# Weight pieces awaited at their first product, attention weights by columns, and new orders on every engine of a transformer block kernel

## The chip, the cores and the metric

One NeuronCore of a Trainium2 chip runs one program. The metric is the device time of one execution in microseconds (us). TensorE multiplies matrices (PE in the rows; PEld is its load of the stationary operand), VectorE (DVE), ScalarE (ACT) and GpSimd (POOL) work elementwise, and SyncE (SP) issues every DMA.

## What is computed

Eight sequences of 256 rows by 256 columns pass through a half-weighted feed-forward layer, an attention layer and a second half-weighted feed-forward layer, each after a layer norm and each added to its input:

```python
x = L0_attn_x                                             # 8 x 256 x 256
x = x + 0.5 * ffn(layernorm(x), w_gate, w_up, w_down)     # hidden 1024, silu(gate) * up
x = x + attn(layernorm(x), gamma, w_qkv, w_out)           # 16 query heads, 4 key heads of 64
x = x + 0.5 * ffn(layernorm(x), w_gate, w_up, w_down)
```

`attn` scales each row to norm 16 with `gamma`, projects to q, k and v (1536 columns), turns q and k by rotary angles, applies a causal softmax, and projects back with `w_out`.

## The kernel before

**Split operands.** Every weight and activation is held as two rounded parts, "hi" and "lo", and a product is three matmuls: hi by hi, lo by hi, hi by lo (`product`, L979). The lo part is a subtraction that ScalarE's rounding copy must precede.

**Work items.** Each engine runs a hand-written list of small functions, one list for the opening (first sequence, and the first layer of the second), one for the loop (six turns; each does the attention of one sequence, the second feed-forward of the same, and the first feed-forward of the next), and one for the ending. On TensorE `gate()`, `up()` and `down()` are twelve matmuls each (L979); pair number F of the hidden layer takes one gate, one up and one down. Four pairs make a layer. `x_transposes` (L988) turn a normed input, `qkv` (opening, ending: by rows) or `qk` and `value_rows` (loop: by columns) are the attention's projections, then come `q_transposes` (opening, ending), `scores`, `p_transposes`, `values` and `projection`.

**Chains between engines.** Feed-forward: gate (PE), `tanh` (ACT, L602), `gate_product` (DVE, L860, which frees the gate's bank and so releases the next gate), up (PE), `up_product` (DVE, L868), `hidden_hi` (ACT, L610), `hidden_lo` (POOL, L436), down (PE). Attention, for eight groups n of four heads: scores, (`low_copy` on ACT, `low_mask` on POOL for the first four groups in the loop), `mask_max` (DVE), `exps` (ACT), `inverse` (DVE), `normalise` (POOL), `p_transposes` (PE), `p_hi` (ACT), `p_lo` (DVE), values (PE), and for two groups together `outputs_hi`, `outputs_lo`, then projection. Layer norm: `statistics` (DVE), `powers` (POOL, four small operations), `normal_rows` (ACT), x_transposes (PE), `x_hi` (ACT), `x_lo` (DVE).

**Rotary.** In the loop `rope_products` (DVE), `rope_add` (POOL), `rope_hi` (ACT) and `rope_lo` (DVE for jobs 0 and 1, POOL for 2 to 4) end in 24 DMAs that restack k and q (`k_restack`, `q_restack` on SP). In the opening and ending `row_products` (DVE) and `row_add` (POOL) precede the q_transposes.

**Weights.** Twelve pieces are loaded into four staging slots: 0 to 3 gate, up, gate, up (first and second half of the hidden layer), 4 and 5 down, 6 to 9 qkv, 10 and 11 out. A piece is rounded by ACT (`split_hi`, L499) and subtracted by DVE (`split_lo`, L673, L675) or, for 4, 5, 10 and 11, by POOL (L342). SP issues piece i when piece i - 4 is subtracted (`lo_done`). TensorE's list has six waits on the counts of finished pieces written into it.

All order comes from these lists and the semaphores between them; nothing is planned at run time.

## Time and profile before

| | before |
|---|---|
| median of 3 runs | 579.34 us (577.7 to 579.7) |
| the profiled execution, own time | 579.26 us |
| its span, first to last instruction | 577.5 us |
| outside the span | 1.8 us |
| TensorE busy / granted clock | 556.5 us (96%) / 0.991 |
| DVE, ACT, POOL busy | 419.9, 379.5, 373.2 us |
| opening / six turns / ending, by first q, k or v product | 99.2 / 397.7 / 80.7 us |

An engine's busy time counts its instructions' modelled spans; matmuls overlap, so two matmuls that start 0.11 us apart are each shown 0.28 us long. Where a wait is shorter than that overlap, only the distance of two starts tells it.

### The profile page before, as it was taken

How to read it: one execution, taken by the hardware profiler on the slowest of the kernel's cores; microseconds unless marked ns; L12 is line 12 of the kernel's file. 1: busy time of each engine (PE TensorE's matmuls, PEld its weight loads, DVE VectorE, ACT ScalarE, POOL GpSimd, SP SyncE). 2: the span in 40 equal slices, each digit the busy share in tenths (PEclk: the TensorE clock that was granted, in tenths of full speed). 3: DMA queues.
4: the chain of work that ended last, by engine and by line, in shares of the span. 5: the costliest groups of instructions: out<-in, count | busy, mean ns of one | idle time of the engine just before them, and what ended most of it. 6: DMA issues, size and time to landing. Idle time of an engine off the chain costs nothing.

```text
span 577.5 us, 13669 instructions
## 1 busy us (share of the span) xinstructions
PE 556.5 (96%) x4364; PEld 528.7 (92%) x4364; DVE 419.9 (73%) x1207; ACT 379.5 (66%) x1013; POOL 373.2 (65%) x410
## 2 busy tenths in 40 slices
PE   7779999999999999999999999999999999899997
PEld 4778999999999999999999999999999999789997
DVE  3686986859867695867867697767868698698533
ACT  4543893479836896379935897368934897479422
POOL 1645562886849775795839875697749877545322
PEclk9897999999999999999999999999999999999999
DMA  7340000250005200160004300070003400000001
GB/s 227 115 132 2 2 1 20 70 151 2 20 18 151 67 18 0 55 182 0 18 18 117 101 17 1 21 200 15 18 18 87 131 0 0 19 1 2 1 1 37
DMA packets 28090, 29.70 MB, mean 51 GB/s; under 512 B 2976, under 2 KB 25888, under 8 KB 28064
## 3 DMA queue, kind: packets, MB, share of 16 engines
q1 hardware_dynamic: 28064, 29.37, 18.3%
q8 instruction: 14, 0.23, 0.2%
q14 instruction: 12, 0.10, 0.1%
HBM read 8.39 MB, written 2.10 MB: 18 GB/s over the span
## 4 chain that ended last, share of the span: by engine, by line
PE 77%; DVE 7%; SPq 5%; issue 4%; ACT 2%; POOL 2%; DMA 2%; POOLq 0%; ACTq 0%; DVEq 0%
PE bank L979 51%; PE bank L988 9%; PE bank L1113 6%; PE bank L1083 5%; SPq L296 3%; PE bank L1108 3%; PE bank L1079 2%; SPq L285 2%; DVE hid L860 1%; DVE q_t L754 1%; ACT hid L602 1%; DMA q_t<-rotated 1%; DMA eye_sb<-in_eye 1%; POOL out_lo L342 1%; DVE qkv_lo L675 1%
## 5 line engine op out<-in xcount | busy, mean ns | idle before, releaser
L427 POOL TENSOR_TENSOR probs<-probs,inv_sum 128x512 f32<-128x512 f32 (+1 forms) x64 | 93.9, 1470 | 54.0 <-DVE inv_sum L828 53.9
L570 ACT ACTIVATE probs<-probs,neg_max 128x128 f32<-128x128 f32 (+1 forms) x256 | 113.2, 450 | 3.9 <-DVE neg_max L818 3.7
L436 POOL TENSOR_TENSOR hid_lo<-hid,hid_hi 128x512 fp32r<-128x512 f32 x64 | 82.8, 1298 | 33.7 <-ACT hid_hi L610 33.0
L979 PE MATMUL bank<-xf_t_hi,gate_hi 128*128 128x256 f32 x256 | 75.1, 293 | 6.9 <-DVE gate_lo L673 3.8
L979 PE MATMUL bank<-down_hi,hid_hi 128*128 128x256 f32 x256 | 72.9, 285 | 1.3 <-POOL hid_lo L436 1.2
L979 PE MATMUL bank<-xf_t_hi,up_hi 128*128 128x256 f32 x256 | 72.9, 285 | 0.0
L979 PE MATMUL bank<-down_hi,hid_lo 128*128 128x256 f32 x256 | 71.8, 280 | 0.0
L979 PE MATMUL bank<-xf_t_hi,up_lo 128*128 128x256 f32 x256 | 71.8, 280 | 0.0
L979 PE MATMUL bank<-down_lo,hid_hi 128*128 128x256 f32 x256 | 71.8, 280 | 0.0
L979 PE MATMUL bank<-xf_t_lo,up_hi 128*128 128x256 f32 x256 | 71.8, 280 | 0.0
L979 PE MATMUL bank<-xf_t_lo,gate_hi 128*128 128x256 f32 x256 | 71.6, 280 | 0.0
L979 PE MATMUL bank<-xf_t_hi,gate_lo 128*128 128x256 f32 x256 | 71.5, 279 | 0.0
L602 ACT ACTIVATE hid<-bank 128x512 f32<-128x512 f32 x64 | 38.2, 597 | 49.7 <-PE bank L979 39.2
L860 DVE SCALAR_TENSOR_TENSOR hid<-hid,bank 128x512 f32<-128x512 f32 x64 | 43.7, 683 | 28.1 <-ACT hid L602 27.8
L979 PEld LDWEIGHTS bank<-xf_t_hi,gate_hi 128*128 128x128 f32 x256 | 48.3, 189 | 10.9 <-DVE gate_lo L673 4.0
L818 DVE CUSTOM_DVE_ANT_0 probs<-bank,mask_sb 128x256 f32<-128x256 f32 (+1 forms) x160 | 55.3, 390 | 0.9 <-PE bank L1083 0.5
L988 PE MATMUL bank<-eye_sb,probs 128*128 128x128 f32 x384 | 52.0, 273 | 0.2
L979 PEld LDWEIGHTS bank<-down_hi,hid_hi 128*128 128x128 f32 x256 | 48.7, 190 | 2.6 <-POOL hid_lo L436 1.6
L446 POOL TENSOR_TENSOR o_t_lo<-o_sums,o_t_hi 128x512 fp32r<-128x512 f32 x24 | 31.1, 1294 | 30.6 <-ACT o_t_hi L595 30.6
L868 DVE TENSOR_TENSOR hid<-hid,bank 128x512 f32<-128x512 f32 x64 | 43.9, 685 | 9.1 <-PE bank L979 6.2
L570 ACT ACTIVATION_READ_ACCUMULATOR probs<-probs,neg_max 128x1 f32 x256 | 49.9, 195 | 0.0
L979 PEld LDWEIGHTS bank<-down_lo,hid_hi 128*128 128x128 f32 x256 | 48.8, 191 | 0.6
(142 smaller groups left out, 1809.3 us busy)
## 6 DMA issues: line engine op xcount, KB each, us to landing
q_t<-rotated SPq DMA_DIRECT2D x96, 128.0 KB, 2.6
k_t<-rotated_k SPq DMA_DIRECT2D x48, 128.0 KB, 2.6
x_in<-in_x SPq DMA_DIRECT2D x7, 256.0 KB, 2.7
out<-y_out SPq DMA_DIRECT2D x7, 256.0 KB, 2.1
probs<-in_w_qkv SPq DMA_DIRECT2D x4, 384.0 KB, 3.7
probs<-in_w_gate SPq DMA_DIRECT2D x2, 512.0 KB, 6.7
probs<-in_w_up SPq DMA_DIRECT2D x2, 512.0 KB, 7.6
probs<-in_w_down SPq DMA_DIRECT2D x2, 512.0 KB, 4.5
```

Of the source, the lines that this page charges most:

```text
L427: nc.gpsimd.tensor_tensor(part, part, inv_sum[:, slot].unsqueeze(2).broadcast_to([P, GROUP, keys]), ALU.mult).then_inc(p_done, 1)
L436: nc.gpsimd.tensor_tensor(hid_lo[:, slot].rearrange("p c n -> p (c n)"), hid[:, slot], hid_hi[:, slot].rearrange("p c n -> p (c n)").bitca ...
L446: nc.gpsimd.tensor_tensor(o_t[1][:, t, jp].rearrange("p g s -> p (g s)"), o_sums[:], o_t[0][:, t, jp].rearrange("p g s -> p (g s)").bitcas ...
L570: last = nc.scalar.activation(part, part, ACT.Exp, bias=neg_max[:, slot, g:g + 1], scale=-1.0, accum_out=row_sum[:, slot, g:g + 1])
L602: nc.scalar.activation(hid[:, slot], bank[G_BANK][:], ACT.Tanh, scale=0.5).then_inc(th_done, 1)
L818: last = nc.vector.tensor_tensor_reduce(part, bank[S_BANKS[pair]][:, g % 2 * SEQ:g % 2 * SEQ + keys], mask_sb[:, SEQ - keys:SEQ] if masked ...
L860: nc.vector.scalar_tensor_tensor(out=hid[:, slot], in0=hid[:, slot], scalar=1.0, in1=bank[G_BANK][:], op0=ALU.add, op1=ALU.mult).then_inc( ...
L868: nc.vector.tensor_tensor(hid[:, slot], hid[:, slot], bank[U_BANK][:], ALU.mult).then_inc(mul_done, 1)
L979: last = nc.tensor.matmul(dst, a[x], b[y], start=start and i == 0, stop=stop and i == 2, skip_group_check=shared)
L988: last = nc.tensor.transpose(t_bank(c)[:, i * P:i * P + P], block_in, eye_sb[:])
L1083: last = nc.tensor.matmul(dst, q_t[:, j, g, t * P:t * P + P], k_t[:, j, s, :], start=s == 0, stop=s == 1)
L1113: last = nc.tensor.matmul(bank[O_BANK][:], value_pair(kb, j), p_t[n % 2][s][:, kb], start=kb == 0 and s == 0, stop=kb == t and s == 1)
```

## The change

The number of arithmetic instructions and their shapes stay. Three things change. `eye` is issued ahead of the first weights, `gamma` and the second input behind piece 4. The pieces of w_qkv go by column halves (both row chunks of columns 0 to 767, then of 768 to 1535) in place of row chunks. TensorE's waits for weights move into the functions: `weight(i)` waits for piece i at the first product that reads it. And all lists are written anew.

```diff
-                   for k in range(KC) for i in (0, width)]
+                   for i in (0, width) for k in range(KC)]
...
             sp.dma_start(x2[:], rows(x, 0)).then_inc(x0_loaded, 16)
+            sp.dma_start(eye_sb[:], eye).then_inc(eye_in, 16)
...
-                if i == W_GATE_UP - 1:
+                if i == 4:
                     sp.dma_start(gamma_sb[:], gamma).then_inc(gamma_in, 16)
                     sp.dma_start(x_in[:], rows(x, 1)).then_inc(x_loaded, 16)
...
+                if c["Q"] in (0, 1):
+                    weight(W_QKV - KC * (2 - c["Q"]) + 1)
...
+            def weight(i):
+                semaphore, count = lo_done(i)
+                pe.wait_ge(semaphore, turn.at(semaphore, count))
             def gate():
                 pe.wait_ge(t_lo, turn.at(t_lo, c["ff"]))
+                if c["F"] < PAIRS and c["F"] % 2 == 0:
+                    weight(c["F"])
```

TensorE's lists begin thus, the opening (the written-out waits are gone), the loop and the ending:

```diff
-            keep_warm(3)
-            pe.wait_ge(eye_in, turn.at(eye_in, 16))
-            keep_warm(3), x_transposes("ff")
...
+            keep_warm(6), x_transposes("ff"), gate(), up(), gate(), up(), gate(), up(), gate(), up(), down(), down()
+            x_transposes("ff"), down(), down(), gate(), up(), gate(), x_transposes("xa"), up(), qkv(0, 0), qkv(0, 1)
...
-                qk(0), qk(1), qk(2), qk(3), x_transposes("ff"), qk(4), value_rows(), gate(), up(), gate(), up()
...
+                qk(0), qk(1), qk(2), qk(3), x_transposes("ff"), qk(4), gate(), value_rows(), up(), gate(), up()
...
-            qkv(0, 0), qkv(0, 1), qkv(0, 2), q_transposes("ending", 0, 0), q_transposes("ending", 0, 1), qkv(1, 0)
...
+            qkv(0, 0), qkv(0, 1), qkv(0, 2), qkv(1, 0), q_transposes("ending", 0, 0), q_transposes("ending", 0, 1)
```

VectorE at the start of the opening, behind the statistics of the first input (gate_lo and up_lo are split_lo of pieces 0 to 3, xf_t_lo is x_lo, hid gate_product on bank5 and up_product on bank6). Before:

```order
L673 TENSOR_TENSOR gate_lo<-probs,gate_hi 128x2x512
L728 TENSOR_TENSOR xf_t_lo<-bank3,xf_t_hi 128x512
L673 TENSOR_TENSOR up_lo<-probs,up_hi 128x2x512
L860 SCALAR_TENSOR_TENSOR hid<-hid,bank5 128x512
L868 TENSOR_TENSOR hid<-hid,bank6 128x512
L860 SCALAR_TENSOR_TENSOR hid<-hid,bank5 128x512
L868 TENSOR_TENSOR hid<-hid,bank6 128x512
L673 TENSOR_TENSOR gate_lo<-probs,gate_hi 128x2x512
L687 BN_STATS stats<-x_in 128x6 x2
L695 BN_AGGR mean_var<-stats 128x2 x2
L673 TENSOR_TENSOR up_lo<-probs,up_hi 128x2x512
```

VectorE at the same place of the changed kernel:

```order
L727 TENSOR_TENSOR xf_t_lo<-bank3,xf_t_hi 128x512
L672 TENSOR_TENSOR gate_lo<-probs,gate_hi 128x2x512
L672 TENSOR_TENSOR up_lo<-probs,up_hi 128x2x512
L672 TENSOR_TENSOR gate_lo<-probs,gate_hi 128x2x512
L859 SCALAR_TENSOR_TENSOR hid<-hid,bank5 128x512
L867 TENSOR_TENSOR hid<-hid,bank6 128x512
L859 SCALAR_TENSOR_TENSOR hid<-hid,bank5 128x512
L867 TENSOR_TENSOR hid<-hid,bank6 128x512
L672 TENSOR_TENSOR up_lo<-probs,up_hi 128x2x512
```

The first piece's subtraction went behind x_lo, the third's ahead of the first products; the fourth's follows the second pair's products directly.

VectorE in the loop, behind rope_products(2) (rope_c and rope_s on bank0 are rope_products(3), L788 is rope_lo(0) and (1)). Before:

```order
L728 TENSOR_TENSOR xf_t_lo<-bank2,xf_t_hi 128x512
L786 REGISTER_ALU
L788 TENSOR_TENSOR rotated_k<-rotated_k 128x512
L786 REGISTER_ALU
L788 TENSOR_TENSOR rotated<-rotated 128x512
L740 REGISTER_ALU
L743 TENSOR_TENSOR rope_c<-bank0,rope_sb 128x512
L743 TENSOR_TENSOR rope_s<-bank0,rope_sb 128x512
```

VectorE at the same place of the changed kernel:

```order
L727 TENSOR_TENSOR xf_t_lo<-bank2,xf_t_hi 128x512
L739 REGISTER_ALU
L742 TENSOR_TENSOR rope_c<-bank0,rope_sb 128x512
L742 TENSOR_TENSOR rope_s<-bank0,rope_sb 128x512
L785 REGISTER_ALU
L787 TENSOR_TENSOR rotated_k<-rotated_k 128x512
L785 REGISTER_ALU
L787 TENSOR_TENSOR rotated<-rotated 128x512
```

Two products went ahead of the two subtractions for which SyncE's restacking DMAs wait. Further on in the same list value_halves moved from behind the mask_max of group 0 to behind that of group 2, right ahead of p_lo of group 0.

GpSimd at the start of the ending (q_rot and k_rot are row_add, the four operations from power_in to shift are powers). Before:

```order
L359 TENSOR_TENSOR power_in<-mean_var,eps_row 128x4
L361 TENSOR_SCALAR less_mean<-mean_var 128x2
L362 TENSOR_TENSOR power_out<-power_in,exponent 128x4
L352 TENSOR_TENSOR shift<-less_mean,power_out 128x2
L395 TENSOR_TENSOR q_rot<-rope_c,rope_s 128x2x4x32 x4
L401 TENSOR_TENSOR k_rot<-rope_c,rope_s 128x4x32 x4
```

GpSimd at the same place of the changed kernel:

```order
L394 TENSOR_TENSOR q_rot<-rope_c,rope_s 128x2x4x32 x4
L358 TENSOR_TENSOR power_in<-mean_var,eps_row 128x4
L360 TENSOR_SCALAR less_mean<-mean_var 128x2
L361 TENSOR_TENSOR power_out<-power_in,exponent 128x4
L351 TENSOR_TENSOR shift<-less_mean,power_out 128x2
L400 TENSOR_TENSOR k_rot<-rope_c,rope_s 128x4x32 x4
```

The powers of the norm stand behind the two q additions instead of ahead of them, and still ahead of the k addition.

## Rows read from the trace of the kernel before

**Rows 1.** The page, part 1: busy time and share of the span.
```profile
PE 556.5 (96%) x4364; PEld 528.7 (92%) x4364; DVE 419.9 (73%) x1207; ACT 379.5 (66%) x1013; POOL 373.2 (65%) x410
```

**Rows 2.** Busy time by stretch: start:end, length, busy of each engine, granted clock, DMA.
```profile
0.00:47.44 47.44, 36.20 (x217) 30.31 (x217) 28.13 (x42) 23.30 (x33) 19.14 (x27) 0.92 0.46 144
47.44:99.16 51.72, 50.97 (x357) 46.52 (x357) 41.79 (x131) 33.55 (x99) 28.70 (x32) 0.98 0.03 7
99.16:496.85 397.69, 394.62 (x3243) 383.29 (x3241) 299.10 (x888) 281.09 (x768) 291.24 (x312) 1.00 0.20 54
496.85:577.50 80.65, 74.74 (x554) 68.61 (x552) 50.90 (x146) 41.58 (x113) 34.16 (x40) 1.00 0.03 11
```

**Rows 3.** Waits of TensorE: releaser, us in total, times, longest.
```profile
PE bank L979 <- DVE gate_lo L673: 3.8, 1, 3.8
PE bank L988 <- ACT xn L506: 3.6, 2, 3.2
PE bank L988 <- POOL q_rot L395: 2.1, 3, 0.8
PE bank L1079 <- DMA q_t<-rotated: 1.5, 4, 0.6
```

**Rows 4.** Timeline of DVE and POOL, opening: start us, us, engine, operation.
```profile
11.75 1.23 DVE L673 TENSOR_TENSOR up_lo<-probs,up_hi 128x1024 fp32r<-128x1024 f32 x1 [0.25 <-ACT up_hi L499]
18.02 2.34 POOL L342 TENSOR_TENSOR down_lo<-probs,down_hi 128x1024 fp32r<-128x1024 f32 x1 [0.55 <-ACT down_hi L499]
18.43 3.02 DVE L673 TENSOR_TENSOR gate_lo<-probs,gate_hi 128x1024 fp32r<-128x1024 f32 x1
39.67 2.32 DVE L717 SCALAR_TENSOR_TENSOR factor<-power_out 128x2 f32<-128x2 f32 x1 [0.73 <-POOL power_out L362]
```

**Rows 5.** Busy time by stretch in the opening, for the granted clock.
```profile
10.00:11.00 1.00, 0.14 (x2) 0.00 (x0) 0.20 (x1) 0.83 (x2) 0.00 (x0) 1.00 1.05 374
23.00:24.00 1.00, 1.00 (x7) 1.00 (x6) 0.50 (x1) 0.50 (x2) 0.92 (x3) 0.50 0.71 267
48.00:49.00 1.00, 1.00 (x4) 0.81 (x3) 0.36 (x1) 0.00 (x0) 1.00 (x1) 0.50 0.00 0
```

**Rows 6.** Timeline of TensorE, opening.
```profile
11.59 0.36 PE L979 MATMUL bank<-xf_t_hi,gate_hi 128*128 128x256 f32 x1 [1.46 <-issue]
43.96 1.12 PE L988 MATMUL bank<-eye_sb,xn 128*128 128x128 f32 x4 [3.23 <-ACT xn L506]
47.44 0.63 PE L979 MATMUL bank<-qkv_hi,xa_t_hi 128*128 128x512 f32 x1
```

**Rows 7.** Timeline of DVE and TensorE, third turn of the loop.
```profile
243.32 0.69 DVE L860 SCALAR_TENSOR_TENSOR hid<-hid,bank 128x512 f32<-128x512 f32 x1 [0.18 <-ACT hid L602]
243.71 0.28 PE L979 MATMUL bank<-xf_t_hi,up_lo 128*128 128x256 f32 x1
244.06 0.38 PE L979 MATMUL bank<-xf_t_hi,gate_hi 128*128 128x256 f32 x1
252.15 0.75 DVE L796 CAST v_parts<-bank 128x256 fp32r<-128x256 f32 x2
252.93 0.76 DVE L801 TENSOR_TENSOR v_parts<-bank,v_parts 128x256 fp32r<-128x256 f32 x2
```

**Rows 8.** Timeline of SP's DMA queue and TensorE, third turn.
```profile
241.36 1.20 SPq L285 DMA_DIRECT2D k_t<-rotated_k  x2
254.71 2.58 SPq L296 DMA_DIRECT2D q_t<-rotated  x4
259.50 0.50 PE L1079 MATMUL bank<-k_t,q_t 128*128 128x256 f32 x2 [0.46 <-DMA q_t<-rotated]
```

**Rows 9.** Timeline of POOL, start of the ending.
```profile
498.79 0.20 POOL L359 TENSOR_TENSOR power_in<-mean_var,eps_row 128x4 f32<-128x4 f32 x1 [4.03 <-DVE mean_var L695]
500.51 2.79 POOL L395 TENSOR_TENSOR q_rot<-rope_c,rope_s 128x256 f32<-128x256 f32 x4
503.26 1.71 POOL L401 TENSOR_TENSOR k_rot<-rope_c,rope_s 128x128 f32<-128x128 f32 x4
```

More of the change, by code:

```diff
@@ L926, in _ @@
                 first_statistics(), rope_products(0), rope_products(1), second_statistics(x2), rope_products(2)
-                x_lo(xf_t), rope_lo(0), rope_lo(1), rope_products(3), gate_product(), up_product(), rope_products(4)
-                gate_product(), up_product(), gate_product(), up_product(), mask_max(0), mask_max(1), value_halves()
-                mask_max(0), mask_max(1), inverse(), gate_product(), x_lo(xf_t), up_product(), mask_max(0)
-                inverse(), mask_max(1), mask_max(0), p_lo(0, 0), inverse(), mask_max(1), gate_product(), mask_max(0)
@@ L936, in _ @@
-                p_lo(6, 0), add_large_half(5), gate_product(), up_product(), p_lo(7, 1), add_large_half(6)
-                p_lo(7, 0), unit_shift(), add_large_half(7), x_lo(xa_t), ffn_residual(y_out, x2)
-                attention_residual(x2, 0), attention_residual(x2, 1)
+                x_lo(xf_t), rope_products(3), rope_lo(0), rope_lo(1), gate_product(), rope_products(4), up_product()
+                gate_product(), up_product(), gate_product(), mask_max(0), mask_max(1), up_product(), mask_max(0)
@@ L939, in _ @@
+                p_lo(4, 0), gate_product(), inverse(), mask_max(0), add_large_half(3), mask_max(1)
+                attention_statistics(), p_lo(5, 1), p_lo(5, 0), add_large_half(4), inverse(), up_product()
+                p_lo(6, 1), p_lo(6, 0), add_large_half(5), unit_shift(), gate_product(), p_lo(7, 1), p_lo(7, 0)
+                up_product(), add_large_half(6), add_large_half(7), ffn_residual(y_out, x2)
+                attention_residual(x2, 0), x_lo(xa_t), attention_residual(x2, 1)
                 c["OT"] += JOBS["OT"]
@@ L1191, in _ @@
-            pe.wait_ge(w_lo_pool, turn.at(w_lo_pool, 2))
-            down(), down(), gate(), up(), gate(), x_transposes("xa"), up()
-            pe.wait_ge(w_lo, turn.at(w_lo, 8))
-            qkv(0, 0), qkv(0, 1), qkv(0, 2), qkv(1, 0), q_transposes("opening", 0, 0), q_transposes("opening", 0, 1)
-            qkv(1, 1), qkv(1, 2), q_transposes("opening", 0, 2), gate()
-            pe.wait_ge(w_lo_pool, turn.at(w_lo_pool, 4))
-            q_transposes("opening", 1, 1), q_transposes("opening", 1, 0), scores(0), scores(1), down(), scores(0)
@@ new lines, in _ @@
+            q_transposes("opening", 0, 2), gate(), q_transposes("opening", 1, 1), q_transposes("opening", 1, 0)
+            scores(0), scores(1), up(), scores(0), scores(1), down(), scores(0), q_transposes("opening", 1, 2)
+            scores(1), scores(0), p_transposes(0, 0), scores(1), down(), scores(0), p_transposes(1, 0), scores(1)
+            values(0), p_transposes(2, 0), scores(0), gate(), scores(1), scores(0), values(1), p_transposes(3, 0)
+            scores(1), scores(0), up(), values(2), p_transposes(4, 1), scores(1), p_transposes(4, 0), down()
@@ L1233, in _ @@
-            up(), down(), down(), x_transposes("ff"), down(), gate(), up(), gate(), up(), gate(), up(), down()
-            gate(), up(), down(), down(), down()
+            qkv(0, 0), qkv(0, 1), qkv(0, 2), qkv(1, 0), q_transposes("ending", 0, 0), q_transposes("ending", 0, 1)
+            qkv(1, 1), q_transposes("ending", 0, 2), x_transposes("ff"), qkv(1, 2), scores(0), scores(1)
+            q_transposes("ending", 1, 0), q_transposes("ending", 1, 1), gate(), scores(0), scores(1), up()
+            q_transposes("ending", 1, 2), scores(0), scores(1), gate(), p_transposes(0, 0), scores(0), scores(1)
@@ new lines, in _ @@
+            up(), scores(0), scores(1), p_transposes(1, 0), values(0), p_transposes(2, 0), scores(0), scores(1)
+            values(1), p_transposes(3, 0), down(), scores(0), scores(1), values(2), p_transposes(4, 0)
+            p_transposes(4, 1), values(3), scores(0), scores(1), gate(), p_transposes(5, 1), p_transposes(5, 0)
+            up(), values(4), p_transposes(6, 1), p_transposes(6, 0), values(5), p_transposes(7, 1)
+            p_transposes(7, 0), values(6), values(7), projection(0, 0), projection(0, 1), projection(1, 0)
```

186 lines of the change are left out of this document (87 added, 99 removed).

## The prediction

> **What bounds the kernel now.** I read the busy shares first, then busy time by stretch, then TensorE's waits, then timelines at the waits. TensorE is busy 556.5 us, 96% of the span; the next engine stands at 73% [rows 1]. Between the first q product of the loop and that of the ending it is busy 394.6 of 397.7 us, 99%; there a new order can return only what hides between matmuls. Up to the first q product, at 47.44, it is busy 36.2 us, at a granted clock of 0.92; in the ending it lacks 80.65 - 74.74 = 5.9 us [rows 2]. Its longest waits lie in the opening: 3.8 us for a gate_lo piece and 3.2 us for the norm ahead of attention; then 2.1 us for row additions and 1.5 us in four waits for restacked q [rows 3]. So the opening decides, the loop is worth tenths of a microsecond, times six, and the ending one or two.
>
> **How the sum is made.** I walked the new lists item by item. An item starts at the latest of its engine's turn and the ends of what it waits for; durations are those of the trace: twelve matmuls 1.4 us (starts 0.114 apart, [rows 7]), tanh 0.6, a product on DVE 0.69 with the next 0.6 after its start, hidden_hi 0.6, hidden_lo 1.3, normal_rows 1.1, powers 1.8; ACT starts 0.25 and DVE 0.2 after the last matmul's slot, other hand-overs take 0.03 to 0.1. Such a walk is exact only where the slack is larger than a tenth or two, so each part gets the walk's value as its best bound and a chosen value nearer to zero.
>
> **Opening.** Before, the third gate waits for piece 2's gate_lo. DVE comes to it at 18.43 and holds it 3.02 us, while up_lo, the same shape, took 1.23. GpSimd was in down_lo from 18.02 to 20.36, and DVE ends 1.1 us after that; a tiny factor operation that took 2.32 us beside GpSimd's next such subtraction shows the same [rows 4]. So a DVE operation that reads only the shared memory waits for GpSimd's whole operation. The Trainium skill, GPSIMD Engine Reference, Specifications, says that the two engines share their memory interfaces and that DVE instructions with two such inputs contend; that names which operations meet, not the length. The rows give the length, and I go by them.
>
> After, TensorE's six warming products run in one go, so the first transposes come some 0.8 us earlier; but x_lo now precedes the first gate_lo, so the first gate starts at 11.8 instead of 11.59 [rows 6]: 0.7 for x_lo and 1.2 for gate_lo from about 9.9. Pieces 1 and 2 are subtracted by 14.0, with GpSimd idle. The pair chain (gate 1.45, hand-over 0.25, tanh 0.63, gate_product 0.72, together 3.05) then sets the second gate at 14.85 and the third at 17.95, where it was at 21.50: 3.6 us won. But piece 3's subtraction comes up at 18.5 and meets GpSimd's down_lo (18.25 to 20.6, since ACT rounds piece 4 at 17.1): it ends at 20.6 + 1.1 = 21.7, and the third up waits from 19.4 to 21.7. So the stall does not vanish: 2.3 us of it move behind the third gate. What then runs is up to 23.2, gate to 24.6, up to 26.1, two downs to 28.9, transposes to 29.3, a down to 30.7, and a down to 32.2 that waits 0.1 for its hidden_lo; x_lo of the second input is done at 31.4. So the fifth gate starts at 32.2, which was at 36.0. The second stall goes from 3.23 us to 1.35: unit_shift no longer runs beside out_lo (its first operation takes 0.15 instead of 2.32), since hidden_lo and a norm stand between. It leaves 1.35 because the norm chain starts at the layer's last down, at 32.4: residual and statistics to 34.1, powers to 35.8, unit_shift to 36.9, normal_rows to 38.0, while TensorE has gate, up and a gate that starts at 35.25, until 36.7. x_lo of the attention input ends at 40.0, and the first q product, which was at 47.44, starts at 40.05. Its weights (pieces 6 and 7, columns 0 to 767) are subtracted by 32.5; pieces 8 and 9, whose subtraction of 0.95 us each stands directly ahead of that x_lo, by 38.9: covered by the 3.5 us from unit_shift's end to x_lo's input. The ordering by columns itself is worth nothing, as all four pieces are in by then; its cover is 1 us.
>
> The clock: it is 1.00 after the idle 1.46 us at 10.13, and 0.50 at 23 to 24, after 3.8 us idle, and at 48 to 49, after 3.2 us idle [rows 5, 6]. At one half it cost: the first low stretch some 3.4 us long, so 1.7 us; the second, about 6.8 us long, 3.4, of which 1.2 lie behind 47.44. After, idle stretches of 2.6 (9.2 to 11.8), 2.3 and 1.35 us stand between the shown cases. If none lowers the clock, the lead at the first transposes of q is 47.44 - 40.05 + 1.2 = 8.6 us; each low stretch of the shorter kind takes 1.7. By the Trainium skill, TensorE: Matmul & The Clock Gate, Part 1, idleness drops the array to half rate; no run here shows it for stretches of this length. I take one short low stretch: 8.6 - 1.7 = **6.9 us**, bounds 4.5 (two, and 0.7 of waits) and 8.6.
>
> From there to the loop TensorE was busy 50.97 of 51.72 us [rows 2], so a lead is passed on. What changes there: out_lo (2.36) moved between row additions, which makes the last of them 1.1 us later relative to TensorE; first needed two score groups later, covered. Fewer downs stand among the last groups; ACT needs 24.5 us from the first exps to the last p_hi, TensorE 28.9 to the same place: covered by 4 us. Nothing is added.
>
> **Loop.** Each turn is 397.7 / 6 = 66.3 us. The visible stalls: the gate after the first and after the second pair, where gate, tanh, gate_product take longer than up: DVE ends at 244.01, and the gate starts 0.35 us after the last matmul where the rhythm is 0.11, so 0.24 each [rows 7]; and group 3's scores, where 24 restacking DMAs in one queue, 0.65 us apart from 241.36 (241.36 to 257.29 for 24), plus a landing of about 2.6 us end at 259.5, 0.46 late [rows 8]; over six turns such waits are 1.5 us [rows 3], with the smaller ones below the listing 0.35 a turn. Together 0.83. After: value_rows between gate and up removes one 0.24, two more matmul groups stand ahead of group 3's scores, so the DMAs' end is covered by 0.9 us even though rope_products(3) ahead of rope_lo delays their start by 0.25 (it fills 0.87 us in which DVE waited); the second 0.25 and 0.05 at the first gate stay. Walk: 0.83 - 0.30 = 0.53 a turn. Against it: in my walk some eight items have under 0.15 us of slack. The tightest is values(0): value_halves, 0.75 + 0.76 = 1.54 us with its gap [rows 7], now stands right ahead of p_lo(0), which ends at 30.2 after the turn's first product, where TensorE wants it at 30.5. I take **0.45 a turn, 2.7 us**; bounds 0 and 0.65 x 6 = 3.9 (the third turn by itself would give 0.9).
>
> **Ending.** TensorE waits about 0.75 us twice for q additions that start only when powers has ended, 500.51 against 498.79 [rows 3, 9]. After, they start 0.6 us earlier, and qkv(1,0), 1.4 us, runs in their place: 1.9 won. But powers, 1.8 us, now delays the k addition to 504.5 + 1.71 = 506.2, when TensorE has wanted it since 504.7: 1.5 lost. Later transposes leave 0.5; more gates and ups among the groups and a down between the last pairs give 0.8 in the walk. Best 1.3; I take **0.9**, bounds -0.5 and 1.3.
>
> **Sum.** 6.9 + 2.7 + 0.9 = 10.5 us, from the profiled execution's own 579.26 us (0.1 below the median): **568.7 us**. At this size no change and a change tell apart at about 0.5%, 2.9 us.
>
> **Rivals.**
> (a) The forecast, one low stretch and most of the loop's gain: 566.5 to 572, chance 0.50.
> (b) The clock never falls, and the walk holds: 579.3 - 8.6 - 3.9 - 1.3 = 565.5. For it: 1.46 us did no harm [rows 5]; against it: 2.6 us is nearer to 3.2 than to 1.46. With 563 to 566.5, chance 0.17.
> (c) The opening's gain alone: the loop was already 99% busy, and the eight tight items of the new list each lose what the removed waits gave: 579.3 - 6.9 = 572.4; with a small loss in loop or ending, or two low stretches, 572 to 576.4. Chance 0.20.
> (d) The change doesn't shorten the opening: the wait for piece 2 becomes that for piece 3 in full, the longer half-clock stretch comes with it, and only the loop and ending act: about 577 to 581. For it: the blocked subtraction is still there; against it: by then a gate more is done. 0.05.
> (e) Slower. In the loop value_halves comes late to its new place. If the masks of group 2 (restack, scores, low_copy, low_mask) come 1.5 us later than I walk, DVE adds 1.54 us behind them, and values(0), the next of TensorE's items with no filler ahead of it, idles 3.0 - 0.3 = 2.7 us in each turn: 6 x 2.7 = 16.2, less 7.8 of opening and ending, 587.7 us. It cancels the gain at 1.3 us a turn and makes a slower kernel, by more than 0.5%, from 1.8. For it: group 3's DMAs are late already; against it: DVE is busy 75% of the loop [rows 2] and waited over 1 us twice near its old place. Chance 0.08.
>
> **Numbers.** (a) is likeliest, so 568.7. The range 564 to 576 leaves out the lower part of (b), most of (d) and (e), about 0.17. Under 576.4 lie (a), (b), (c): 0.87; within 0.5% 0.05; slower 0.08.
>
> **What would show it.** Right: the third gate near 18 with a wait of about 2.3 us now in front of the third up; the wait for xn down to 1.4; the first q product between 40 and 42.5; turns of 65.7 to 65.9 us; no wait for q_t DMAs; one wait of about 1.5 us for k_rot in the ending in place of the two for q_rot. Wrong: granted clock at 0.50 twice or more in the opening; turns at or above 66.3, with a wait of TensorE for p_even_lo or p_odd_lo, hid, or o_sums inside the loop; a DVE operation of the opening that GpSimd holds at another place than piece 3's.

## The result, and the profile of the changed kernel

The changed kernel takes **585.99 us** (median of 5 runs, 584.12 to 587.37) against 578.6 us (577.32 to 579.7) beside it: a ratio of 1.0125, 95% interval 1.0091 to 1.0158. I had forecast 568.7 and gave "slower" a chance of 0.08. The profiled execution took 584.12 us, 4.9 above that of the kernel before, while the medians are 7.4 apart: the granted clock fell more often in three of the five executions (mean 0.991 and twice 0.994, against 0.997 in the profiled one and in one other), while the profiled execution of the kernel before had 0.991.

Busy time of the changed kernel by stretch, cut at the same four places as [rows 2]; the columns are start:end, length, busy time with the number of instructions of PE, PEld, DVE, ACT and POOL, granted clock, DMA share and GB/s:

```profile
0.00:41.87 41.87, 34.13 (x216) 28.48 (x216) 24.24 (x42) 22.88 (x33) 17.35 (x27) 0.96 0.50 163
41.87:93.30 51.43, 49.85 (x357) 45.40 (x358) 41.93 (x132) 34.06 (x99) 30.38 (x32) 1.00 0.02 7
93.30:502.12 408.82, 397.20 (x3242) 384.46 (x3241) 312.45 (x888) 286.89 (x768) 288.57 (x312) 1.00 0.20 54
502.12:582.30 80.18, 74.08 (x554) 68.19 (x552) 51.14 (x146) 41.45 (x113) 34.11 (x40) 1.00 0.02 8
```

Read the lengths first. Against [rows 2] the first q product comes 5.57 us earlier and the stretch to the loop is 0.29 shorter; the ending is 0.47 shorter. The loop is 408.82 us where it was 397.69: **11.13 us longer, 1.85 in each turn**. The sum, -5.86 + 11.13 - 0.47 = +4.8, is the difference of the two spans. VectorE's column is the hint: in the loop it is busy 13.35 us more, with the same 888 instructions.

TensorE's waits, the answer to [rows 3] (releaser, us in total, times, longest; "..." stands for rows that the text does not use):

```profile
PE bank L1116 <- DVE o_sums L834: 10.3, 6, 1.7
PE bank L978 <- issue: 2.6, 1, 2.6
PE bank L978 <- DVE up_lo L672: 2.0, 1, 2.0
PE bank L987 <- ACT xn L505: 1.8, 3, 1.1
...
PE bank L987 <- POOL k_rot L400: 1.3, 1, 1.3
...
```

The first row is new: six waits of 1.7 us, one a turn, for an addition into o_sums. L1116 is `values` in the loop (the product of a group's attention weights with v), L834 is `add_large_half` on VectorE, which `values` waits for.

VectorE's groups of instructions between 93.3 and 502.12 (shapes, count, then busy us and mean ns, then idle before): two of them have only two elements a partition and still take over 1.2 us each.

```profile
L716 DVE SCALAR_TENSOR_TENSOR factor<-power_out 128x2 f32<-128x2 f32 x6 | 7.7, 1278 | 0.2
L718 DVE TENSOR_SCALAR factor<-factor 128x2 f32<-128x2 f32 x6 | 7.3, 1222 | 0.2
L719 DVE RECIPROCAL factor<-factor 128x2 f32<-128x2 f32 x6 | 1.0, 166 | 0.2
```

These are the first three of the five small operations of `unit_shift`, which turn GpSimd's powers into the factor and shift of the norm ahead of attention. The third turn shows what lies around them. Timeline of VectorE, from add_large_half(5) to add_large_half(6):

```profile
283.95 0.69 DVE L834 TENSOR_TENSOR o_sums<-o_sums,bank 64x512 f32<-64x512 f32 x1
284.67 1.28 DVE L716 SCALAR_TENSOR_TENSOR factor<-power_out 128x2 f32<-128x2 f32 x1
285.98 1.22 DVE L718 TENSOR_SCALAR factor<-factor 128x2 f32<-128x2 f32 x1
287.24 0.17 DVE L719 RECIPROCAL factor<-factor 128x2 f32<-128x2 f32 x1
...
287.82 0.69 DVE L859 SCALAR_TENSOR_TENSOR hid<-hid,bank 128x512 f32<-128x512 f32 x1
288.43 1.28 DVE L727 TENSOR_TENSOR p_odd_lo<-bank,p_odd_hi 128x512 fp32r<-128x512 f32 x2
289.63 0.67 DVE L867 TENSOR_TENSOR hid<-hid,bank 128x512 f32<-128x512 f32 x1
290.22 0.67 DVE L834 TENSOR_TENSOR o_sums<-o_sums,bank 64x512 f32<-64x512 f32 x1
```

Timeline of GpSimd in the same microseconds:

```profile
284.65 1.28 POOL L435 TENSOR_TENSOR hid_lo<-hid,hid_hi 128x512 fp32r<-128x512 f32 x1 [0.55 <-ACT hid_hi L609]
285.89 1.29 POOL L445 TENSOR_TENSOR o_t_lo<-o_sums,o_t_hi 128x512 fp32r<-128x512 f32 x1
```

TensorE, with the wait ahead of values(7):

```profile
288.97 0.28 PE L978 MATMUL bank<-out_hi,o_t_lo 128*128 128x256 f32 x1
290.95 0.50 PE L1116 MATMUL bank<-p_odd_hi,v_parts 128*128 128x512 f32 x1 [1.71 <-DVE o_sums L834]
```

GpSimd's hidden_lo ends at 285.93, the first tiny operation at 285.95; GpSimd's outputs_lo ends at 287.18, the second tiny operation at 287.20. unit_shift, 0.8 us of work, takes 3.1. Behind it in VectorE's queue stand gate_product, both p_lo of group 7, up_product and add_large_half(6), and for the last TensorE's values(7) waits from 289.2 to 290.9. In the kernel before, unit_shift stood behind p_lo(7,0) and nothing that TensorE wanted soon was queued behind it. In its third turn it started 0.6 us after GpSimd's last subtraction had ended. VectorE, then GpSimd, in the kernel before:

```profile
291.57 0.14 DVE L717 SCALAR_TENSOR_TENSOR factor<-power_out 128x2 f32<-128x2 f32 x1
```

```profile
289.66 1.30 POOL L436 TENSOR_TENSOR hid_lo<-hid,hid_hi 128x512 fp32r<-128x512 f32 x1
```

The opening, where I had foreseen the same effect, for piece 3, first in VectorE's timeline:

```profile
18.60 0.69 DVE L859 SCALAR_TENSOR_TENSOR hid<-hid,bank 128x512 f32<-128x512 f32 x1 [1.30 <-ACT hid L601]
...
20.00 3.06 DVE L672 TENSOR_TENSOR up_lo<-probs,up_hi 128x1024 fp32r<-128x1024 f32 x1
```

GpSimd's timeline there:

```profile
19.60 2.38 POOL L341 TENSOR_TENSOR down_lo<-probs,down_hi 128x1024 fp32r<-128x1024 f32 x1 [0.27 <-ACT down_hi L498]
```

down_lo ends at 21.98 and up_lo 1.08 later, so the third up waits 2.0 us (forecast 2.3). Stretches of one microsecond for the granted clock, which stands behind the busy times:

```profile
10.00:11.00 1.00, 0.00 (x0) 0.00 (x0) 0.93 (x2) 1.00 (x3) 0.00 (x0) 1.00 0.17 66
14.00:15.00 1.00, 1.00 (x6) 1.00 (x6) 0.16 (x1) 0.54 (x2) 0.00 (x0) 0.50 0.61 164
44.00:45.00 1.00, 1.00 (x6) 0.80 (x6) 1.00 (x3) 0.00 (x0) 0.00 (x0) 1.00 0.00 0
```

The clock is at 0.50 in one stretch only, from about 12.5 to 16, behind the 2.6 us in which TensorE has nothing to do ahead of the first gate.

### The profile page after: what moved, and what is told of

It reads as the page before. It is cut to its first block, busy times and chain, and to the rows that moved or that the text cites. A ratio compares the mean times of both kernels' runs of the same rounds, so it can differ in the third digit from the quotient of the medians.

```text
span 582.3 us, 13665 instructions
## 1 busy us (share of the span) xinstructions
PE 555.3 (95%) x4364; PEld 526.5 (90%) x4364; DVE 429.8 (74%) x1207; ACT 385.3 (66%) x1013; POOL 370.4 (64%) x410
## 4 chain that ended last, share of the span: by engine, by line
PE 76%; DVE 12%; issue 5%; ACT 3%; POOL 2%; DMA 0%; POOLq 0%; DVEq 0%; ACTq 0%
PE bank L978 52%; PE bank L987 8%; PE bank L1116 5%; PE bank L1086 5%; PE bank L1111 3%; PE bank L1082 2%; DVE hid L859 2%; DVE factor L716 1%; PE bank L973 1%; DVE q_t L753 1%; DVE factor L718 1%; ACT hid L601 1%; DVE o_sums L834 1%; PE bank L1078 1%; DVE p_odd_lo L727 1%
## 5 line engine op out<-in xcount | busy, mean ns | idle before, releaser
L978 PE MATMUL bank<-down_lo,hid_hi 128*128 128x256 f32 x256 | 71.4, 279 | 0.0
L978 PE MATMUL bank<-down_hi,hid_lo 128*128 128x256 f32 x256 | 71.4, 279 | 0.0
L978 PEld LDWEIGHTS bank<-xf_t_hi,up_hi 128*128 128x128 f32 x256 | 48.9, 191 | 2.5 <-DVE up_lo L672 2.2
L609 ACT ACTIVATE hid_hi<-hid 128x512 fp32r<-128x512 f32 x64 | 40.6, 634 | 15.9 <-DVE hid L867 12.6
L978 PEld LDWEIGHTS bank<-xf_t_lo,up_hi 128*128 128x128 f32 x256 | 48.7, 190 | 0.3
```

The lines of the kernel that those rows point to most:

```text
L609: nc.scalar.activation(hid_hi[:, slot].rearrange("p c n -> p (c n)"), hid[:, slot], ACT.Copy).then_inc(h_hi, 1)
L978: last = nc.tensor.matmul(dst, a[x], b[y], start=start and i == 0, stop=stop and i == 2, skip_group_check=shared)
```

## The experiments

My theory after the result: **unit_shift's new place, beside GpSimd's subtractions, makes the 10.3 us**, by way of VectorE's queue. The rivals: the new loop lists are tight everywhere (value_halves ahead of p_lo(0), for one), and would lose the same time at another item; or ScalarE's queue, where small_half(6) now stands behind normal_rows, is what is late. Each experiment has its expectation, written before it ran, and then its result. Turns are counted between the first q products of two turns, from the second turn on; the first is up to 0.9 us longer in the changed kernel and in experiments 1 to 3.

**1. unit_shift back behind add_large_half(6).**

```diff
-  add_large_half(5), unit_shift(), gate_product(), p_lo(7, 1), ..., add_large_half(6), add_large_half(7)
+  add_large_half(5), gate_product(), p_lo(7, 1), ..., add_large_half(6), unit_shift(), add_large_half(7)
-  p_hi(7, 0), normal_rows(x1_next, True), small_half(6)          (ScalarE)
+  p_hi(7, 0), small_half(6), normal_rows(x1_next, True)
```

> The changed kernel with the end of its loop turn put back in two places: VectorE's unit_shift stands behind add_large_half(6) instead of ahead of gate_product, and ScalarE's small_half(6) stands ahead of normal_rows(x1_next). My theory (the loop lost 1.85 us a turn because unit_shift meets GpSimd's subtractions, its first two tiny operations take 1.28 and 1.22 us, and gate_product, both p_lo(7), up_product and add_large_half(6) queue behind it, so values(7) waits 1.71 us): that wait is gone or below 0.3 us, the two operations take 0.15 and 0.17 us, turns fall from 68.07 to 66.1 to 66.7 us (a wait of some 0.4 us for hid_lo at the turn's last down may appear, since hidden_hi now stands behind a later normal_rows), 573 to 576 us in all. Rival (the new lists are tight everywhere, value_halves ahead of p_lo(0) among them, and TensorE loses the same time at the next tight item): turns stay at 67.5 us or above, time above 581 us.

Measured 577.36 us (ratio 0.9985, 0.9959 to 1.001, the same as before), 8.6 below the changed kernel; turns 66.7 to 67.1. The wait for o_sums is gone from the list, and the two operations take as little as the other three:

```profile
L718 DVE TENSOR_SCALAR factor<-factor 128x2 f32<-128x2 f32 x6 | 1.0, 170 | 0.2
L716 DVE SCALAR_TENSOR_TENSOR factor<-power_out 128x2 f32<-128x2 f32 x6 | 0.9, 146 | 0.0
```

The wait for hid_lo that I had expected came, 0.5 us in each turn, and I had it too small: turns lie above my 66.1 to 66.7 us and the time 1.4 us above my 576. "Tight everywhere" falls for 7.0 of the loop's 11.1 us: the loop is 401.8.

**2. unit_shift where GpSimd stands still.**

```diff
-  add_large_half(4), inverse(), up_product(), p_lo(6, 1), p_lo(6, 0), add_large_half(5), unit_shift(), gate_product()
+  add_large_half(4), unit_shift(), inverse(), up_product(), p_lo(6, 1), p_lo(6, 0), add_large_half(5), gate_product()
```

> The changed kernel with VectorE's unit_shift moved ahead, between add_large_half(4) and the inverse behind it, where GpSimd has nothing to do until that inverse has run; ScalarE's and GpSimd's lists as they are. If the length of unit_shift comes from GpSimd's running subtraction: its first two operations fall from 1.28 and 1.22 to 0.15 and 0.17 us, the wait for o_sums at values(7) vanishes, GpSimd's last normalise starts about 0.9 us later and costs TensorE 0.3 to 0.6 us at p_transposes(7), turns 66.4 to 66.9 us, 574 to 578 us. If the length is the operations' own in this place (their operands, or VectorE's queue): they stay at 1.2 us each, and the time stays at 582 us or above.

Measured 576.31 us, ratio 0.995 (0.9934 to 0.9966); turns 66.7 to 66.9 from the second on. Timeline of VectorE in the third turn:

```profile
281.90 0.14 DVE L716 SCALAR_TENSOR_TENSOR factor<-power_out 128x2 f32<-128x2 f32 x1
282.08 0.17 DVE L718 TENSOR_SCALAR factor<-factor 128x2 f32<-128x2 f32 x1
```

And of GpSimd:

```profile
280.49 1.02 POOL L361 TENSOR_TENSOR power_out<-power_in,exponent 128x4 f32<-128x4 f32 x1
283.01 1.90 POOL L426 TENSOR_TENSOR probs<-probs,inv_sum 128x1024 f32<-128x1024 f32 x1 [1.50 <-DVE inv_sum L827]
```

The same operations, earlier in the same queue, take 0.14 and 0.17 us, since between 281.5 and 283.0 GpSimd runs nothing. Their length is not their own. The price was not where I expected it: no wait at p_transposes(7), but up_product, 0.7 us later in the turn, holds the next up for 0.33 us a turn.

**3. Only ScalarE's order put back.**

```diff
-  p_hi(7, 0), normal_rows(x1_next, True), small_half(6)
+  p_hi(7, 0), small_half(6), normal_rows(x1_next, True)
```

> The changed kernel with one edit on ScalarE alone: small_half(6) ahead of normal_rows(x1_next), VectorE's list as it is. My theory (VectorE's own queue sets add_large_half(6): it comes up at 290.22 in the third turn whatever ScalarE does): small_half(6) runs 2.6 us earlier, values(7) still waits 1.5 to 1.7 us, turns 68.0 to 68.1, 584 us, no difference. Rival (small_half(6), held behind normal_rows that waits 1.55 us for the shift, is what makes add_large_half(6) late): the wait falls below 0.7 us and turns to 67 us, 578 us.

Measured 585.81 us, ratio 1.0106 (1.0083 to 1.0129), turns 68.0 to 68.2 and a wait for o_sums of 1.8 us: no difference. small_half(6) moved 1.75 us forward relative to the turn (it then waits for an outputs_lo of GpSimd, so not by 2.6), and add_large_half(6) not at all. Where two engines are both late, only the last one to let go counts.

**4. The loop of the kernel before** on all five engines, opening and ending as changed.

> The changed kernel with the loop lists of the kernel before on all five engines; opening and ending stay as changed. If opening, loop and ending add up, as in my forecast: turns back to 66.3 us, 584.1 - 11.1 = 573.0 us (572 to 574.5), that is 5.9 us of the opening and 0.5 us of the ending below the kernel before. Rival (the changed loop owes part of its loss to the state in which the changed opening hands over, a shorter lead of the other engines): the first turns stay above 66.8 us and the time above 576 us.

Measured **574.06 us**, ratio 0.9905 (0.9883 to 0.9927), loop 397.99 us. The three parts add up. Note what experiments 1 and 2 leave: with unit_shift mended, the new loop takes 401.8 or 401.4 us, the old one 398.0. Of the difference 3.0 and 2.0 us are the waits that those two edits brought with them.

**5. The waits alone.** Experiment 4 with the opening lists of the kernel before; TensorE's wait for each piece, the order by columns and the early identity stay. (The kernel before has eight waits for pieces written into TensorE's list, not the six of the description.)

```diff
-  keep_warm(6), x_transposes("ff"), gate(), up(), gate(), up(), gate(), up(), gate(), up(), down(), down()
+  keep_warm(3), (wait for the identity), keep_warm(3), x_transposes("ff"), gate(), up(), gate(), up()
+  gate(), down(), up(), gate(), up(), down(), x_transposes("ff"), down(), down(), ...
```

> The kernel with the loop of the kernel before, the changed ending, and now also the opening lists of the kernel before on TensorE, VectorE, ScalarE and GpSimd; of the changed opening there remain TensorE's wait for each weight piece at its first product, the order of the attention pieces by columns, and the earlier transfer of the identity. My theory (the 5.9 us of the opening come from where VectorE subtracts pieces 0 to 2 and from the norm chain, not from the waits): the third gate waits for piece 2 again, 3.0 to 3.8 us, first q product at 46 to 47.5, 577.5 to 579.3 us. Rival (the old waits, each for a count in front of a block, held TensorE back): the first q product comes before 44 and the time is below 576 us.

Measured 580.03 us, ratio 1.0011 (0.9995 to 1.0026), first q product at 47.56, third gate waiting 3.8 us for gate_lo; the time is 0.7 us above my range. A finer wait gives nothing while what it waits for comes no earlier.

**6. Piece 3 subtracted earlier**, on experiment 4.

```diff
-  gate_product(), up_product(), gate_product(), up_product(), split_lo(3), gate_product()
+  gate_product(), up_product(), split_lo(3), gate_product(), up_product(), gate_product()
```

> The kernel with the loop of the kernel before and the changed opening and ending, and one edit: VectorE subtracts piece 3 (up_lo) ahead of the second gate_product instead of behind the second up_product, while GpSimd has nothing to do. My theory: up_lo falls from 3.06 to 1.2 us and the third up's wait of 2.0 us goes; the norm of the second input is then what is late (GpSimd's powers stand behind its second down_lo whatever happens here), so a wait of 1.5 to 2 us appears at the second x_transposes, and 0.6 to 0.9 us are left: 573.3 us beside 574.1 (or 572.0 against 572.9 for runs with the same clock). Rival 1: the 2.0 us are won in full, first q product 2 us earlier, 572 us. Rival 2: up_lo takes 3 us here too, since its length is its own or GpSimd's hidden_lo meets it.

Measured 573.62 us, ratio 0.9885 (0.9843 to 0.9926). Timeline of VectorE in the opening:

```profile
17.75 1.22 DVE L672 TENSOR_TENSOR up_lo<-probs,up_hi 128x1024 fp32r<-128x1024 f32 x1
```

And of GpSimd:

```profile
18.58 1.55 POOL L435 TENSOR_TENSOR hid_lo<-hid,hid_hi 128x512 fp32r<-128x512 f32 x1 [12.06 <-ACT hid_hi L609]
```

up_lo takes 1.22 us instead of 3.06. Now GpSimd, which begins while VectorE is at work, is the longer one: 1.55 instead of 1.28 us. The wait for up_lo goes and that for xn grows from 1.8 to 2.7 us in all, as expected. Experiments 4 and 6 can't be told apart by their medians; of the runs with a mean clock of 0.997, two each, it is 571.6 and 572.8 here against 572.6 and 573.2 there, which overlap.

**7. Powers behind the k addition in the ending**, on experiment 4.

```diff
-  row_add("ending", 0, 0), row_add("ending", 0, 1), powers(), row_add("ending", 0, 2)
+  row_add("ending", 0, 0), row_add("ending", 0, 1), row_add("ending", 0, 2), powers()
```

> The kernel with the loop of the kernel before and the changed opening and ending, and one edit: in the ending GpSimd's powers stands behind the addition for k instead of ahead of it. My forecast had said that powers ahead of it takes back 1.5 of 1.9 us. By that the wait for k_rot (1.3 us) goes; the norm is ready 0.5 us later, and a wait for xn of about 0.6 us comes, 0.7 us left: 573.4 us beside 574.1, ending 79.5 us instead of 80.2. Rival: the later row additions cost as much as is won, ending 80.2 or longer.

Measured 575.71 us, ratio 0.9927 (0.9902 to 0.9952); the ending is 80.16 us, 80.03 in experiment 4: nothing won. The wait for k_rot is gone from the list; in its place stand 0.9 us for a q_lo of VectorE, whose bank the k transposes want (it was 0.4), and 1.0 for xn. I had named the second and not the first, and together they take it all: the rival was right, and my 573.4 us was 2.3 too low. Both waits stood right behind the one removed.

**8. Two more warming products** behind the first transposes, on experiment 4.

```diff
-  keep_warm(6), x_transposes("ff"), gate()
+  keep_warm(6), x_transposes("ff"), keep_warm(2), gate()
```

> The kernel with the loop of the kernel before and the changed opening and ending, and two more warming products of TensorE behind the first transposes, where it idles 2.6 us before its first gate. If that idle stretch is what lowers the granted clock to 0.50 for the first gate and up (they take 2.2 us each where others take 1.4): the clock stays at 1.00, the second gate starts 1.4 us earlier, and the opening with all behind it is 1.0 to 1.6 us shorter, 572.6 us beside 574.1. If the clock falls for another reason (the weight load that begins then, or time since the start): it falls all the same, and the time stays at 574.

Measured 573.84 us, ratio 0.9899 (0.9863 to 0.9935). Two stretches of one microsecond of experiment 4:

```profile
14.00:15.00 1.00, 1.00 (x7) 1.00 (x6) 0.75 (x1) 0.47 (x1) 0.00 (x0) 0.50 1.01 250
25.00:26.00 1.00, 1.00 (x7) 1.00 (x7) 0.00 (x0) 0.00 (x0) 1.00 (x1) 0.50 0.69 233
```

The same two of this kernel:

```profile
14.00:15.00 1.00, 1.00 (x11) 0.99 (x9) 0.85 (x2) 1.00 (x2) 0.00 (x0) 1.00 0.93 213
25.00:26.00 1.00, 1.00 (x7) 1.00 (x7) 0.90 (x4) 0.00 (x0) 0.53 (x1) 0.50 0.70 271
```

With the idle 2.6 us cut to 0.9 the clock stays at 1.00 for the first gate and up. In its profiled execution it fell after the 2.0 us wait of the third up, though, as it had done in experiment 4 and had not in the changed kernel's. My 572.6 us was missed: the median is that of experiment 4, and all four runs, at a mean clock of 0.997, take 573.7 to 574.6 where the two runs of experiment 4 at that clock took 572.6 and 573.2. By itself the edit gains nothing that these runs show.

**9. unit_shift moved, in the kernel before.** One call in its loop, nothing else:

```diff
-  add_large_half(5), gate_product(), up_product(), p_lo(7, 1), add_large_half(6), p_lo(7, 0), unit_shift(), add_large_half(7)
+  add_large_half(5), unit_shift(), gate_product(), up_product(), p_lo(7, 1), add_large_half(6), p_lo(7, 0), add_large_half(7)
```

> The kernel before, with one edit in its loop: VectorE's unit_shift stands behind add_large_half(5), as in the changed kernel, instead of behind p_lo(7,0); nothing else is changed. If that place is enough to lose the time: in the third turn unit_shift would start at 287.3, beside GpSimd's hidden_lo (to 288.45) and outputs_lo (to 289.7); its first two operations take about 1.1 and 1.2 us, and add_large_half(6) and p_lo(7,0) end at 293.6 where TensorE wants values(7) at 291.8: a wait of 1.2 to 1.8 us a turn, turns 67.3 to 68, 586 to 590 us. Rival (it needs the other new orders too): turns within 0.3 us of 66.1, 579 to 581 us.

Measured **599.73 us**, ratio 1.0343 (1.0324 to 1.0363): 20 us slower. Timeline of VectorE in its fourth turn:

```profile
365.17 1.03 DVE L717 SCALAR_TENSOR_TENSOR factor<-power_out 128x2 f32<-128x2 f32 x1
366.24 1.23 DVE L719 TENSOR_SCALAR factor<-factor 128x2 f32<-128x2 f32 x1
```

Of GpSimd:

```profile
364.90 1.28 POOL L436 TENSOR_TENSOR hid_lo<-hid,hid_hi 128x512 fp32r<-128x512 f32 x1
366.15 1.29 POOL L446 TENSOR_TENSOR o_t_lo<-o_sums,o_t_hi 128x512 fp32r<-128x512 f32 x1
```

And the first of TensorE's waits:

```profile
PE bank L1113 <- DVE p_odd_lo L728: 15.7, 6, 2.7
```

The place alone is enough, and it costs more here than I had walked (2.6 us at values(7), not 1.2 to 1.8, and 599.7 us, not 586 to 590): in this kernel ScalarE has a hidden_hi ahead of small_half(6), so the delay runs over up_product, hidden_hi and small_half(6) and back to VectorE. The stall of 2.6 us also brings low-clock stretches into the loop, in three of its six turns. Behind the first of them:

```profile
162.00:165.00 3.00, 2.94 (x10) 2.56 (x11) 0.38 (x1) 0.97 (x2) 0.00 (x0) 0.55 0.00 0
```

All six turns are 68.9 to 71.4 us.

**10. Attention pieces by rows again**, on experiment 4: the first q product waits for all four.

> The kernel with the loop of the kernel before and the changed opening and ending, and the four attention weight pieces by rows again, so that TensorE's first q product waits for all four. I had given the order by columns nothing, since all four are subtracted before the input of attention is there: no difference, 574.1 us, first q product at the same place. Rival (the last subtraction stands directly ahead of x_lo and holds the first product back): 1 us or more slower.

Measured 574.5 us, ratio 0.9919 (0.9889 to 0.9949), first q product at 44.11 (44.05 in experiment 4): no difference. Part of the change's description, the order by columns, moves nothing.

**11. Piece 3 and the warming products together**, on experiment 4.

> The loop of the kernel before, the changed opening and ending, and the two opening edits that were tried apart: piece 3 subtracted ahead of the second gate_product, and two more warming products behind the first transposes. If the two add up (0.6 us each in runs of one clock, and no half-clock stretch left in the opening, where both kernels had one or two): first q product at 39.5 to 40.5 us, 570.5 to 572.5 us. Rival (the clock falls at another stall, as it did after the third gate when the first stretch was filled): 573 to 575.

Measured **571.4 us** (570.83 to 571.76), ratio 0.9863, interval 0.9847 to 0.9879: the best version. First q product at 39.90, granted clock 1.00 in the whole profiled execution, and its four runs scatter by less than 1 us, where the four of experiment 4 scatter by 2.7. The busy shares of its page, TensorE first:

```profile
PE 554.0 (97%) x4368; PEld 525.6 (92%) x4368; DVE 414.7 (73%) x1207; ACT 379.5 (67%) x1013; POOL 371.2 (65%) x410
```

**12. The norm of the second input brought forward as well**, on experiment 11.

```diff
-  split_lo(4), hidden_lo(), split_lo(5), powers(), hidden_lo()                     (GpSimd)
+  split_lo(4), hidden_lo(), powers(), split_lo(5), hidden_lo()
-  split_hi(6), split_hi(7), hidden_hi(), normal_rows(x_in), hidden_hi()            (ScalarE)
+  split_hi(6), split_hi(7), normal_rows(x_in), hidden_hi(), hidden_hi()
```

> As the one before with piece 3 and warming edits together, and the norm of the second input brought forward: GpSimd's powers ahead of its second down_lo, ScalarE's normal_rows(x_in) ahead of two hidden_hi. If the chain of that norm is what TensorE waits for at the second x_transposes (1.2 us): that wait goes, hidden_lo of the third pair comes 1 us later and takes most of it back, 0.3 to 0.5 us faster than the one before. Rival: the later hidden_lo costs more than the norm gives, 0.5 us slower.

Measured 572.54 us, ratio 0.9883 (0.9861 to 0.9905): not faster, first q product at 40.51. x_lo of the second input did come 1.2 us earlier, but waits for hid_lo of 2.3 us take the place of 0.7, and piece 5, subtracted 2.9 us later (from 25.54 instead of 22.66), frees its stage later, so that ScalarE waits 2.5 us for the transfer of a later piece ahead of the attention norm. That is what the rival said, and its half a microsecond fits; but the six runs scatter from 570.2 to 574.4, so that the two kernels are not told apart.

## Why the prediction was wrong

**Loop: the step that failed.** I had taken 0.45 us a turn as won; 1.85 were lost. That is 13.8 of the 15.4 us between the forecast and the profiled execution; the opening adds 1.0 and the ending 0.4. Two things are in it: an overlap that I took as free, and a gain that was not there.

The larger is a wait that my walk had as nothing. I walked the end of the turn with unit_shift at its length in the kernel before, about 0.15 us an operation, "durations are those of the trace", and checked value_halves as the tightest item. Yet [rows 4], in my own opening part, shows this operation at 2.32 us beside GpSimd, and I even counted its new cover there as a gain. I did not ask the same question in the loop, where it moved the other way: from a gap of GpSimd into two of its subtractions. Its price is 1.28 + 1.22 - 0.32 = 2.2 us a turn, of which values(7) shows 1.71, 10.3 us over six turns. Experiments 1, 2 and 9 show in turn that the wait goes when the place is changed, that the length comes from GpSimd, and that the place alone is enough; experiment 3 rules out ScalarE's queue.

The smaller is the gain itself. Take the 10.3 us off, and the new loop is 398.5 us where the old one is 397.7: the 2.7 us are not there. Some of it was, since no wait for q_t appears in the list, as forecast. But the first gate now stands right behind qk(4), with value_rows after it instead of before it, and x_lo is later than I walked: in the third turn 0.39 us lie between the starts of the last matmul (237.18) and of the gate (237.57), 0.27 above the rhythm, where I had 0.05. The rest is small items that I did not measure one by one, so their cause stays open.

The Trainium skill has a rule for which operations meet, in GPSIMD Engine Reference, Specifications: GpSimd's interface to the shared memory is contended by VectorE instructions that read two such inputs or run in a two-port mode. By that rule unit_shift's first operation, with two inputs, is held; the trace agrees: L716 took 1.28 us. The rule names nothing else, and here too the trace agrees: stats, two operations with one input each, take 0.75 us beside a subtraction of GpSimd, the first begun 0.02 us before it and the second inside it, and the two that follow lie wholly inside it and take 0.25. L718, with one tensor input, is held; whether it ran in a two-port mode, no run shows (timelines of VectorE and, below it, of GpSimd, third turn):

```profile
278.79 0.75 DVE L686 BATCH_NORM_STATS2 stats<-x_next 128x6 f32<-128x256 f32 x2
279.64 0.25 DVE L694 BATCH_NORM_AGGREGATE mean_var<-stats 128x2 f32<-128x6 f32 x2
```

GpSimd:

```profile
278.81 1.30 POOL L445 TENSOR_TENSOR o_t_lo<-o_sums,o_t_hi 128x512 fp32r<-128x512 f32 x1 [0.30 <-ACT o_t_hi L594]
```

So the prediction's sentence that a VectorE operation that reads only the shared memory waits for GpSimd's whole operation is too wide on VectorE's side. It is too wide on GpSimd's side as well: rope_lo on VectorE, a subtraction with both inputs in the shared memory, begins inside GpSimd's power_out in five of the six turns and takes its usual 0.7 us. VectorE, then GpSimd, third turn:

```profile
238.55 0.68 DVE L787 TENSOR_TENSOR rotated_k<-rotated_k 128x512 fp32r<-128x512 f32 x1
```

```profile
238.47 1.02 POOL L361 TENSOR_TENSOR power_out<-power_in,exponent 128x4 f32<-128x4 f32 x1
```

Every hold of VectorE that these texts count, in the loop and in the opening, is beside a subtraction of GpSimd; By the rule above rope_lo, with its two inputs, would have met power_out as well; the measurement decides, and why it did not stays open.

**Rival (e) had the sign, not the place.** It named the mechanism of a late item in VectorE's queue with TensorE behind it, and the threshold (1.3 us a turn cancels, 1.8 is slower by more than 0.5%): with 1.85 lost the profiled execution was slower by 0.8%, the ratio of the medians by 1.25%. But there is no wait for p_even_lo in the trace; value_halves was not late. A chance of 0.08 for one named item was too low because the other seven tight items had no rival of their own. value_halves at its old place was not tried.

**Opening: right in the profiled execution, a little too large.** 5.86 of 6.9 us. The wait moved from piece 2 to piece 3 and took 2.0 us (2.3), the wait for xn fell to 1.1 (1.35), the first q product came at 41.87, inside 40 to 42.5, and one short low-clock stretch was there. What failed in size is the part behind the first q product, where I had 1.2 us from the old low stretch and "nothing is added": it is only 0.29 us shorter, since TensorE waits 1.5 us there (0.65 for q_rot, 0.55 for o_t_lo, 0.31 for neg_max), where it had waited 0.6 before. Experiment 5 shows that the lists made the gain and the waits none; experiment 10 that the order by columns is worth the zero I gave it.

**Ending: right in mechanism, half in size.** 0.47 of 0.9 us, with the wait for k_rot at 1.3 (1.5) in place of the two for q_rot.

**The case for the clock.** I had one low stretch in the sum and none in the best bound. In the opening there are one or two, depending on the execution: behind the idle 2.6 us the clock always fell, behind the 2.0 us of the third up in most executions. From the start of the third up to the first q product it is 18.76 us in the changed kernel's profile and 20.37 in experiment 4's, with the same lists, so the second costs 1.6 us. That the profiled execution had just the one of my sum is luck: with the same lists up to there (in experiment 10 but for the order by rows), the first q product came at 41.87 and 41.41 in the changed kernel and experiment 1, with one low stretch, and at 43.95 to 44.33 in experiments 2, 3, 4, 7 and 10, with two, where only 3.1 to 3.5 us are won on the 47.44 of before.

A further low stretch, which the prediction does not name, can come in the ending, behind the wait of 1.33 us for k_rot. It did in the profiled executions of experiments 3, 5 and 6, and did not in the eight others that have this wait. TensorE in experiment 6, and its granted clock 2 us behind that:

```profile
500.76 0.66 PE L987 MATMUL bank<-eye_sb,k_rot 128*128 128x128 f32 x4 [1.33 <-POOL k_rot L400]
```

```profile
503.00:504.00 1.00, 1.00 (x4) 0.81 (x3) 1.00 (x2) 0.34 (x1) 0.95 (x2) 0.50 0.00 0
```

So "1.46 us did no harm" was no bound for what is harmless. In experiments 4, 6, 7 and 10 the runs with the lower mean clock are the slower ones, so part of the spread is of this kind. Experiment 11, which cuts the first stall to 0.9 us and removes the second, has little spread in four runs; experiment 12, with the same two cured, still scatters by 2.5 us among its four runs at 1.00, so the clock is not all of it.

## What to carry to other kernels

When a list moves a VectorE operation that has all its inputs in the shared memory, look up what GpSimd runs at the new place, in every stage. Beside a GpSimd subtraction, give the operation GpSimd's remaining time on top of its own (the statistics, with one input, were free of this here); a tiny one can cost a subtraction's length twice over if it stands in front of what TensorE needs. If an effect has been found in one part of a kernel, go through every other moved item with it before a sum is made. And a wait removed is worth the distance to the next one behind it: three of the edits here (the ending's powers, piece 3 alone, the second norm) moved a wait of 1 to 2 us by one item and gained next to nothing that the runs can show.

## What the runs showed of the hardware

- Beside a GpSimd subtraction, VectorE's two-element operations end 0.02 to 0.03 us after it, wherever they begin in it (started at 284.67 and 365.17 beside subtractions that ended at 285.93 and 366.18, they ended at 285.95 and 366.20). TENSOR_SCALAR with one tensor input is held too, 1.22 us; the statistics (0.75 us for two) are not. Beside GpSimd's power_out of 1.02 us a 128x512 subtraction of VectorE is not held either (0.68 us).
- It holds the other way as well: a hidden_lo that began inside VectorE's up_lo took 1.55 us instead of 1.28 (experiment 6), and one in the changed kernel, begun at 22.32 inside the up_lo that ended at 23.06, took 1.89.
- A large VectorE operation still has nearly all its work to do when GpSimd ends: up_lo, begun 0.40 us after down_lo, ended 1.08 us after it, where it takes 1.22 alone.
- The granted clock fell to 0.50 (1.2 GHz) behind the idle stretch of 2.6 us in all eight profiled executions whose opening has it, behind three of the six stalls of 2.5 to 2.7 us in the loop of experiment 9, behind the 2.0 us of the third up in six of eight, and behind 1.33 us in the ending in three of eleven. It stayed at 1.00 (2.4 GHz) for the first gate in the three where the 2.6 us were cut to 0.9.
